# Four-layer transformer on one core: the fourth layer's after-attention work moved into its attention loop, and three projections restaged chunk by chunk

## The chip, the cores and the metric

The kernel runs on one core of one Trainium2 chip. The metric is the time of one execution in microseconds (us) of the device. Engines are named as the profile names them: PE is TensorE, DVE is VectorE, ACT is ScalarE, POOL is GpSimd and SP is SyncE, which here only issues DMAs.

## The reference

Four pre-norm layers over x of shape (4, 1024, 128): a batch of 4, 1024 tokens each, 128 features. Each layer is `x = x + attention(layernorm(x))` and then `x = x + ffn(layernorm(x))`. The fourth layer, which changes most, computes:

```python
q, k = (x @ Wq.T), (x @ Wk.T)            # 8 heads x 2 halves x 8 features
v = x @ Wv.T                             # 8 heads x 16 features
L1, L2 = l2norm(q1) @ l2norm(k1).T * cos_scale, l2norm(q2) @ l2norm(k2).T * cos_scale
G = tanh(delta_gain * (L1 - L2))
y = (softmax(L1 + G) - lambda_full * softmax(L2 - G)) @ v
y = y * rsqrt(mean(y * y over 16) + 1e-5) * subln_weight * 0.5
x = x + y @ Wo.T + bo
# ffn: top-1 of 8 experts, capacity S // E, first come first served
gates = softmax(layernorm(x) @ wg); expert = argmax(gates)
pos = cumsum(one_hot(expert)) - 1; keep = pos < C
out = (relu(xe @ w1 + b1) @ w2 + b2)[slot] * gate
```

The first layer has causal attention of 16 heads, the second an attention with a gain and biases before and in its projection, the third a causal attention of 8 heads and a top-1 mixture of experts like the fourth's.

## The kernel before, in words

x stays in SBUF as `x_sb`, 32 tiles of 128 tokens. Work runs in blocks (`nc.Block()`), each with one hand-written instruction list per engine; the order of every queue is the order in the code, and counting semaphores tie the lists together. A block ends when all its engines have ended. Stages around the change:

- `project` (L114), layers 1 and 2. A loop over four batches; each has two chunks of 512 tokens. DVE normalises the chunks (L107), PE turns them (four transposes), ACT copies them out, PE makes the q and the k product of a chunk (L213) and the v products. Each product is split into three bf16 parts: DVE copies it from PSUM with its bias to `val` (L283, L287), ACT makes the high part (L242), DVE the remainder `val - high` (L295), ACT the middle part (L245), POOL the low part (L259). SP stores parts (L184) and the padded values `vpad` (L187). DVE starts the norms of batch 0 after waiting for all weights and POOL's `vpad` presets.
- `project_cosine` (L1472), layer 4: the same with a third product and l2 norms. A batch's four q and k products are squared by ACT (L1578), summed by DVE (L1612), rooted by ACT (L1580), refined by DVE (L1624 to L1636), turned by PE (L1565), and only then the six splits of that batch run (`val` L1647 and L1649, L1585, L1655, L1588, L1600, stores L1522 and L1525). ACT alternates between Copy/Square (L1575, L1578) and Sqrt (L1580), one set of table loads each batch.
- `cosine_attention` (L1664), layer 4. 256 steps: 4 batches x 4 groups of heads x 2 halves of queries x 8 key blocks. A step s: PE makes the product of the difference (L1757 `a_diff_ps`), ACT takes tanh (L1805 `a_gate`), PE makes two logit products (`a_logit_ps`), DVE adds or subtracts the gate (L1852, two instructions), ACT takes exp of all four tiles a step later (L1811), PE multiplies with v two steps later (L1781). Every eighth step DVE copies the result out (L1847, a step with s % 8 = 2), PE turns it (L1791, s % 8 = 3) and DVE normalises it (L1832, L1834, L1840, s % 8 = 4) into `nat`. Batch 0 is unrolled, batches 1 to 3 are one `Fori(1, BATCH)` whose body is 64 steps.
- Behind it, each for all 32 tiles at once: `out_project` (L1281: square L1355, mean L1374, root, scale L1384, turn, product with Wo L1347, bias L1389, add to x L1395, statistics L42), `layer_stats` (L45), `route` (L1862: transposes L1889, router product L1900), `assign_slots` (L2279), `send_rows` (L2386: 32 indirect DMAs by POOL, L2409, and the load of the expert weights), then `switch_experts` (rows loaded at L2457).
- Layer 3's `row_attention` (L445) already does the same chain for a batch during the next batch's steps (product L608, choice L842 to L852, slots L858 to L880, scatters L643). Its steps are unrolled.

Of the kernel before, what the change touches and what calls it, by code (L numbers as in the profile page):

```python
# [8 lines left out]
U32 = mybir.dt.uint32  # L9
ALU = mybir.AluOpType  # L10
# [11 lines left out]
KB = T // P  # L22
GROUPS = 4
# [90 lines left out]
def project(nc, name, src, mv, rstd, wq, wk, wv, qs, ks, vs, ident, heads, v_width,  # L114
            gain=None, qk_bias=None, v_bias=None, pos=None):

    q_tiles = wq.shape[1] // P
    items = 2 * q_tiles
    vdim = wv.shape[1]
    hd = vdim // heads
    v_items = vdim // P
    with ExitStack() as ctx:
# [9 lines left out]
        w_qk = sb("w_qk", [P, items, P])  # L138
        w_v = sb("w_v", [P, vdim])
        xn = [sb(f"xn{i}", [P, CH]) for i in range(2)]  # L140
        xnT = sb("xnT", [P, 2, CH])
        NB = 4
        val = [sb(f"val{i}", [P, CH]) for i in range(NB)]
        rem = [sb(f"rem{i}", [P, CH]) for i in range(NB)]
        parts = [sb(f"parts{i}", [P, 3, CH], BF16) for i in range(NB)]
        vpad = [sb(f"vpad{i}", [P, CPT, heads, v_width]) for i in range(2)]
        gain_sb = sb("gain_sb", [P, 2])
        bias_sb = sb("bias_sb", [P, items])
        vb_sb = sb("vb_sb", [P, vdim])
        pos_sb = sb("pos_sb", [P, T])  # L150
# [3 lines left out]
        xn_done = sem("xn_done")  # L154
        loaded, xT_ready, xT_done = sem("loaded"), sem("xT_ready"), sem("xT_done")
        item_ready, val_done, hi_done = sem("item_ready"), sem("val_done"), sem("hi_done")
        rem_done, mid_done, lo_done = sem("rem_done"), sem("mid_done"), sem("lo_done")
        v_ready, v_done, v_preset = sem("v_ready"), sem("v_done"), sem("v_preset")
        stored = [sem(f"stored{i}") for i in range(NB)]
        v_stored = [sem(f"v_stored{i}") for i in range(2)]  # L160
        n_loads = 3 + sum(a is not None for a in (gain, qk_bias, v_bias, pos))
# [3 lines left out]
        def _(sp):  # L165
            sp.dma_start(w_qk[:, 0:q_tiles, :], wq.rearrange("c (n d) -> c n d", d=P)).then_inc(loaded, 16)
# [6 lines left out]
            if v_bias is not None:  # L173
                sp.dma_start(vb_sb[:], v_bias.to_broadcast([P, vdim])).then_inc(loaded, 16)
            if pos is not None:
                sp.dma_start(pos_sb[:], pos).then_inc(loaded, 16)
# [2584 lines left out]
```

## Time and profile before

| | |
|---|---|
| median of 3 runs | 3845.98 us (3845.41 to 3851.53) |
| profiled execution, its own time | 3840.85 us |
| span in the profile | 3839.1 us, mean granted clock of PE 0.89 |
| PE busy | 3039.5 us (79%) |
| DVE busy | 2681.6 us (70%) |
| ACT busy | 2180.8 us (57%) |
| POOL busy | 285.7 us (7%) |

Shares of the whole span say little here, since the stages have different limits; the stages the change touches lie in these stretches (us from the span's start):

| stretch | stage |
|---|---|
| 35.5 to 108.9 | `project` of layer 1 |
| 971.0 to 1044.2 | `project` of layer 2 |
| 2704.2 to 2829.3 | `project_cosine` |
| 2829.3 to 3603.8 | `cosine_attention` |
| 3603.8 to 3741.7 | its last turn, then `out_project` to `send_rows` |
| 3741.7 to 3839.1 | `switch_experts` of layer 4 |

A row of the timeline has start, duration, engine, line, operation, out<-in and count; a bracket at the end has the engine's idle time before it and what ended that. `PEld` is the loading of weights into PE, which overlaps its matmuls.

### The profile page before, as it was taken

Reading aid. Unit: us, or ns where it says so; the run is one execution under the profiler, and the core shown is the slowest. Engines: PE = TensorE matmul, PEld = TensorE weight load, DVE = VectorE, ACT = ScalarE, POOL = GpSimd, SP = SyncE. Lnnn points to the kernel's source line nnn. Section 1 sums busy time; section 2 is a strip of 40 time slices with the busy share of each in tenths; the row PEclk is TensorE's granted clock in tenths of the full one; section 3 lists DMA queues with packets and bytes.
Section 4 is the critical chain, followed back from the end, with each engine's and each line's share of the span. In section 5 each row is a group of like instructions: output and inputs, shape, how many; then the busy total and the mean of one; then the engine's idle time right before and its main releaser. Section 6 shows DMA issues by size and latency. Waiting matters only on the chain. (4 is left out here: it accounts for less than half of the span.)

```text
span 3839.1 us, 54232 instructions
## 1 busy us (share of the span) xinstructions
PE 3039.5 (79%) x18410; PEld 1243.4 (32%) x18410; DVE 2681.6 (70%) x5914; ACT 2180.8 (57%) x2753; POOL 285.7 (7%) x347
## 2 busy tenths in 40 slices
PE   3699996796499999996599999956339998989626
PEld 2233334342212222223355555544312222222224
DVE  5799983445599999993566666631658888888721
ACT  2266664222237777775255545522349999999602
POOL 2000000000200000000000000013120000000033
PEclk8699997898669999998699999978669999999858
DMA  6432210000422111200000000012253222220022
GB/s 228 100 54 47 47 26 2 21 0 0 164 49 36 35 29 32 40 1 5 28 1 1 1 6 3 5 52 66 74 110 53 31 31 31 31 31 1 2 72 86
DMA packets 159647, 156.48 MB, mean 41 GB/s; under 512 B 46424, under 2 KB 126056, under 8 KB 156848
## 3 DMA queue, kind: packets, MB, share of 16 engines
q1 hardware_dynamic: 155312, 145.57, 17.6%
q0 software_dynamic: 4096, 7.78, 0.6%
q8 instruction: 144, 2.36, 0.3%
q14 instruction: 95, 0.78, 0.1%
HBM read 91.17 MB, written 62.00 MB: 40 GB/s over the span
## 5 line engine op out<-in xcount | busy, mean ns | idle before, releaser
L1197 ACT ACTIVATE a_probs<-a_scores 128x1024 f32<-128x1024 f32 (+3 forms) x896 | 791.9, 933 | 397.4 <-PE a_scores L1094 247.6
L1220 DVE TENSOR_REDUCE a_part_max<-a_slot_ps 128x1 f32<-128x512 f32 x1280 | 798.6, 684 | 40.3 <-PE a_slot_ps L1072 38.8
L1852 DVE TENSOR_TENSOR a_probs<-a_logit_ps,a_gate 128x1024 f32<-128x1024 f32 x512 | 603.0, 1220 | 116.9 <-ACT a_gate L1805 116.9
L1072 PE MATMUL a_slot_ps<-a_k_op,a_q_op 48*128 48x512 bf16 (+3 forms) x1792 | 579.8, 380 | 113.5 <-DMA a_k_op<-scratch_k 51.6
L1811 ACT ACTIVATE a_probs<-a_probs 128x2048 f32<-128x2048 f32 x256 | 487.7, 1905 | 0.7 <-DVE a_probs L1852 0.7
L1094 PE MATMUL a_scores<-a_q_op,a_k_op 51*128 51x512 bf16 (+3 forms) x1792 | 453.2, 362 | 7.3 <-ACT a_probs L1197 6.1
L1114 PE MATMUL a_o_ps<-a_probs,a_v_op 128*32 128x512 f32 (+3 forms) x3584 | 438.0, 561 | 1.2 <-ACT a_o_sb L1184 0.6
L1072 PEld LDWEIGHTS a_slot_ps<-a_k_op,a_q_op 48*128 48x128 bf16 x1792 | 150.4, 94 | 715.5 <-DVE a_part_max L1220 468.9
L1757 PE MATMUL a_logit_ps<-a_q_op,a_k_op 96*128 96x512 bf16 x1024 | 303.5, 384 | 63.1 <-DVE a_probs L1852 51.3
L1805 ACT ACTIVATE a_gate<-a_diff_ps 128x1024 f32<-128x1024 f32 x256 | 261.2, 1020 | 60.4 <-PE a_diff_ps L1757 49.9
L1781 PE MATMUL a_o_ps<-a_probs,a_v_op 128*32 128x512 f32 x2048 | 274.5, 608 | 2.6 <-ACT a_probs L1811 2.0
L1216 DVE CUSTOM_DVE_ANT_0 a_slot_ps<-a_slot_ps,a_mask_wide 128x128 f32<-128x128 f32 (+3 forms) x512 | 237.0, 516 | 14.2 <-PE a_slot_ps L1072 13.2
L670 ACT ACTIVATE a_turned_sb<-a_turn_ps 128x512 f32<-128x512 f32 x192 | 93.6, 487 | 211.2 <-PE a_turn_ps L545 210.6
L660 ACT ACTIVATE space<-space,a_lows 128x128 f32<-128x128 f32 (+7 forms) x256 | 195.2, 768 | 4.0 <-DVE a_lows L754 4.0
L1757 PE MATMUL a_diff_ps<-a_qd_op,a_k_op 96*128 96x512 bf16 x512 | 156.2, 387 | 41.9 <-DMA a_v_op<-scratch_v 37.3
L545 PE MATMUL a_turn_ps<-ident_sb,space 128*128 128x128 f32 x1152 | 168.0, 278 | 21.6 <-DVE a_turned_sb L765 16.9
L765 DVE COPY a_turned_sb<-a_turn_ps 128x512 f32<-128x512 f32 x192 | 106.7, 556 | 94.7 <-PE a_turn_ps L545 94.2
L754 DVE CUSTOM_DVE_ANT_0 space<-a_score_ps,a_mask 128x512 f32<-128x512 f32 (+3 forms) x256 | 138.6, 587 | 37.7 <-PE a_score_ps L532 37.5
L1757 PEld LDWEIGHTS a_logit_ps<-a_q_op,a_k_op 96*128 96x128 bf16 x1024 | 78.7, 97 | 251.8 <-DVE a_probs L1852 206.4
L545 PEld LDWEIGHTS a_turn_ps<-ident_sb,space 128*128 128x128 f32 x1152 | 133.3, 142 | 69.3 <-issue 32.1
L532 PE MATMUL a_score_ps<-a_kT,a_qT 64*128 64x512 f32 (+3 forms) x768 | 153.2, 519 | 1.1 <-DVE a_lows L754 1.0
L559 PE MATMUL a_o_ps<-a_turned_sb,a_v 128*64 128x512 f32 (+3 forms) x768 | 149.6, 511 | 0.0
(398 smaller groups left out, 3782.5 us busy)
## 6 DMA issues: line engine op xcount, KB each, us to landing
a_q_op<-scratch_q SPq DMA_DIRECT2D x576, 32.0 KB
a_k_op<-scratch_k SPq DMA_DIRECT2D x576, 32.0 KB
scratch_v<-p_vpad SPq DMA_DIRECT2D x16, 1024.0 KB, 4.6
a_v_op<-scratch_v SPq DMA_DIRECT2D x32, 512.0 KB, 6.4
scratch_q<-p_parts SPq DMA_DIRECT2D x24, 384.0 KB, 2.6
scratch_k<-p_parts SPq DMA_DIRECT2D x24, 384.0 KB, 2.6
a_qd_op<-scratch_g SPq DMA_DIRECT2D x192, 32.0 KB
slots<-zero_slots SPq DMA_DIRECT2D x2, 2080.0 KB, 8.7
```

Source lines behind the costliest of these rows:

```text
L545: mm = nc.tensor.transpose(turn_ps[j][:, t * P:(t + 1) * P], rows_of(u, h, t)[0][:, j, kb * P:(kb + 1) * P], ident[:])
L1072: nc.tensor.matmul(out[:, 0:width], q_op[g][r0:r0 + MAX_ROW, e, qt * P:(qt + 1) * P], k_op[g][r0:r0 + MAX_ROW, e, kh * CH:kh * CH + width] ...
L1094: return nc.tensor.matmul(scores[e][:, jj, off:CH], k_op[g][r0:r1, e, kb * P:(kb + 1) * P], q_op[g][r0:r1, e, hq * CH + off:(hq + 1) * CH] ...
L1114: mm = nc.tensor.matmul(o_ps[32 * j:32 * (j + 1), off:CH], v_op[g][:, kb, 32 * j:32 * (j + 1)], probs[(u * S + n) % NB][:, j, off:CH], sta ...
L1197: nc.scalar.activation(probs[gs % NB][:, 2 * e:2 * e + 2, off:CH], scores[e][:, :, off:CH], ACT.Exp, scale=scale).then_inc(probs_done, 1)
L1216: nc.vector.tensor_tensor_reduce(out=slot[:, 0:w], in0=slot[:, 0:w], in1=mask_wide[:, CH - w:CH], scale=1.0, scalar=-3e38, op0=ALU.add, op ...
L1220: nc.vector.tensor_reduce(part_max[u % 2][:, kh, col:col + 1], slot[:, 0:w], axis=AX.X, op=ALU.max).then_inc(slot_done, 1)
L1757: mm = nc.tensor.matmul(out[:, j, :], ops[g][0][:, j, kb * P:(kb + 1) * P], q[:, j, hq * CH:(hq + 1) * CH], start=True, stop=True)
L1781: mm = nc.tensor.matmul(o_ps[c0:c0 + 32, :], v_op[g][:, kb, j * 32:(j + 1) * 32], probs[s2 % 4][:, m, j, :], start=kb == 0, stop=kb == KB - 1)
L1805: nc.scalar.activation(gate[s % 2][:], diff_ps[:], ACT.Tanh).then_inc(gate_done, 1)
L1811: nc.scalar.activation(tile[:], tile[:], ACT.Exp).then_inc(exp_done, 1)
L1852: nc.vector.tensor_tensor(probs[s % 4][:, m, :, :], logit_ps[m][:], gate[s % 2][:], op) \
```

## The change

1. `project`: no loops. The steps of chunk c and the transposes of chunk c + 2 are interleaved. The copy to `val` is gone: ACT makes the high part straight from PSUM (with the bias), DVE the remainder from PSUM. `parts` has 8 buffers for 4, `vpad` 4 for 2 (POOL presets four). DVE makes the norms of four chunks before it waits for the presets and the weights.
2. `project_cosine`: the same, with products, squares, roots and norms of chunk c + 1 made while chunk c is split. One Sqrt and its reciprocal and refinement for each chunk (128 elements) where there was one for each batch (256).
3. `cosine_attention`: the loop over batches is unrolled to 256 steps and 64 more behind them. At step r of the next batch, work of the finished batch runs: DVE means at r = 7, PE turns at 13 and 15 (ACT copies a step later), PE products with Wo at 17 and 20, DVE adds to x at 18 and 21, statistics at 19 and 22, moments at 23, PE turns at 30 and 32, router product at 34, DVE choice at 35, 37, 38, ACT exp at 36, PE counts at 39, DVE slots at 40 to 43. All PE tasks of this kind and the turns of L1791 share one PSUM bank, `spare_ps`. POOL adds the output bias to all of x at the start and, for each batch, squares, takes the inverse roots (17 small instructions each, twice), scales, makes the eight normalised row tiles and issues the eight scatters.
4. `out_project`, `layer_stats`, `route`, `assign_slots` and `send_rows` of layer 4 are gone. The expert weights load into the space of the attention's operands of groups 0 and 1 once the last batch has left them.

The core of the diff (of project: one product; of the attention: the new lists):

```diff
 def project(...):
-                for n in range(2 * items + 1):
-                        nc.scalar.activation(parts[n % NB][:, 0, :], val[n % NB][:], ACT.Copy).then_inc(hi_done, 1)
+            for c in range(CHUNKS):
+                high(2 * c)
+                if c > 0:
+                    middle(2 * c - 1)
+                high(2 * c + 1)
+                middle(2 * c)
+                if c + 2 < CHUNKS:
+                    take(c + 2)
+            for c in range(4):
+                norm(c)
+            dve.wait_ge(v_preset, 8)
             dve.wait_ge(loaded, 16 * n_loads)
+            for c in range(CHUNKS):
+                remainder(2 * c)
+                remainder(2 * c + 1)
+                values_out(c)
+                if c + 4 < CHUNKS:
+                    norm(c + 4)
 def project_cosine(...):   # DVE
+            for c in range(CHUNKS):
+                if c + 1 < CHUNKS:
+                    sums(c + 1)
+                remainder(ITEMS * c)
+                if c + 3 < CHUNKS:
+                    norm(c + 3)
+                remainder(ITEMS * c + 1)
+                if c + 1 < CHUNKS:
+                    units(c + 1)
+                remainder(ITEMS * c + 2)
+                if c + 1 < CHUNKS:
+                    values_out(c + 1)
 def cosine_attention(...):
-            steps(0, range(NS))
-            with te.Fori(1, BATCH) as b:
-                steps(b, range(NS))
+            for gs in range(shape.END):
...
+                for task in shape.tasks(gs):
+                    spare(task)
+        at = {13: ("t", 0), 15: ("t", 1), 17: ("y", 0), 20: ("y", 1), 30: ("x", 0), 32: ("x", 1), 34: ("l",), 39: ("n",)}
+            def inverse_root(v, y, y0, trial, factor):   # POOL
+                root(nc.gpsimd.tensor_scalar(first, bits, -0.5, float(0x5f3759df), ALU.mult, ALU.add))
+                for i in range(4):
+                    root(nc.gpsimd.tensor_tensor(trial, y0, y0, ALU.mult))
+                    root(nc.gpsimd.tensor_tensor(trial, trial, v, ALU.mult))
+                    root(nc.gpsimd.tensor_scalar(trial, trial, -0.5 * last, 1.5 * last, ALU.mult, ALU.add))
+                    root(nc.gpsimd.tensor_tensor(y if i == 3 else y0, y0, trial, ALU.mult))
+            for b in range(BATCH):   # POOL
+                pool.wait_ge(nat_done, 2 * GROUPS * (b + 1))
+                nc.gpsimd.tensor_tensor(square[:], rows, rows, ALU.mult).then_inc(squared, 1)
+                pool.wait_ge(mean_done, b + 1)
+                inverse_root(mean[:], inv[:], guess[:], trial[:], 0.5)
+                nc.gpsimd.tensor_tensor(groups, groups, inv[:].unsqueeze(2).to_broadcast([P, NG, RMS]), ALU.mult).then_inc(scaled, 1)
+                pool.wait_ge(moments, b + 1)
+                inverse_root(var[:], rstd[:], var_guess[:], var_trial[:], 1.0)
+                for t in range(KB):
+                    ins = nc.gpsimd.tensor_scalar(xr[:, t, 0:D], x[:, tile * D:(tile + 1) * D], mv[:, t, 0:1], rstd[:, t:t + 1], ...)
+                pool.wait_ge(slot_done, b + 1)
+                for t in range(KB):
+                    nc.gpsimd.indirect_dma_start(out=slots, ...).then_inc(sent[b], 16)
 def four_layers(...):
-                out_project(nc, "o3", nat, D, a["L3_Wo"], x, stats, consts, bias=a["L3_bo"], rms=(16, 1e-5, 0.5, a["L3_subln"]))
-                layer_stats(nc, "f3n", x, mv, rstd, dst=xn, stats=stats)
-                route(nc, "f3r", xn, a["L3_wg"], EXPERTS, logits, ident)
-                assign_slots(nc, "f3a", logits, descending[EXPERTS], a["before_me"], gate, slot_in)
-                send_rows(nc, "f3s", xn, slot_in, gate, a["token_ids"], slots[1], sent, weights.load)
```

## Rows read from the trace of the kernel before

**Rows 1.** Windows, one for each stage: busy us of each engine (x instructions).

```profile
core 0: us, PE busy (x) PEld busy (x) DVE busy (x) ACT busy (x) POOL busy (x), PEclk, DMA share, GB/s
35.50:108.90 73.40, 38.43 (x128) 23.21 (x128) 40.74 (x72) 23.90 (x41) 23.86 (x21) 0.78 0.60 225
971.00:1044.20 73.20, 38.76 (x128) 23.33 (x128) 41.63 (x72) 25.43 (x40) 24.08 (x20) 0.69 0.55 204
2704.20:2829.30 125.10, 51.59 (x288) 46.13 (x288) 91.44 (x144) 55.70 (x85) 35.48 (x29) 0.61 0.32 111
2829.30:3603.80 774.50, 679.75 (x3708) 163.15 (x3708) 649.07 (x638) 712.32 (x513) 10.50 (x6) 0.98 0.23 31
3603.80:3741.70 137.90, 34.45 (x198) 32.51 (x198) 52.50 (x159) 17.70 (x22) 30.98 (x32) 0.58 0.17 50
3741.70:3839.10 97.40, 65.56 (x352) 45.47 (x352) 17.34 (x28) 25.98 (x40) 31.09 (x32) 0.83 0.30 86
```

**Rows 2.** Timeline of the attention: tanh gates eight steps apart, and the turn.

```profile
3044.41 1.02 ACT L1805 ACTIVATE a_gate<-a_diff_ps 128x1024 f32<-128x1024 f32 x1 [0.20 <-PE a_diff_ps L1757]
...
3047.12 1.01 ACT L1805 ACTIVATE a_gate<-a_diff_ps 128x1024 f32<-128x1024 f32 x1
...
3049.41 0.66 PE L1791 MATMUL a_turn_ps<-ident_sb,a_o_sb 128*128 128x128 f32 x4
...
3050.53 1.02 ACT L1805 ACTIVATE a_gate<-a_diff_ps 128x1024 f32<-128x1024 f32 x1 [0.59 <-PE a_diff_ps L1757]
...
3067.47 1.02 ACT L1805 ACTIVATE a_gate<-a_diff_ps 128x1024 f32<-128x1024 f32 x1
```

**Rows 3.** The same view of the stores of the first projection.

```profile
50.00:106.00 56.00, 31.56 (x108) 19.06 (x106) 36.71 (x62) 21.56 (x37) 19.97 (x16) 0.73 0.67 252
```

**Rows 4.** Tiles of the projections: ns min/median/max, first and last start.

```profile
L295 DVE TENSOR_TENSOR p_rem<-p_val,p_parts x32: 675/681/1464, 49.4 to 1032.9; 128x512 f32<-128x512 f32 x32
L1655 DVE TENSOR_TENSOR p_rem<-p_val,p_parts x24: 674/834/1636, 2726.3 to 2820.2; 128x512 f32<-128x512 f32 x24
...
L312 DVE TENSOR_TENSOR p_vpad<-p_v_ps,p_vb_sb x8: 678/684/693, 984.8 to 1034.3; 128x512 f32<-128x512 f32 x8
...
L1575 ACT ACT_TABLE_LOAD  x4: 1283/1283/1283, 2704.8 to 2794.0; - x4
```

**Rows 5.** Groups of lines between the attention and the experts' first load.

```profile
L2409 POOL DMA_INDIRECT slots<-f_xn,f_slot_in x32 | 31.0, 968 | 866.0 <-DVEq L2388 856.5 <-issue 9.1 <-DMA slots<-f_xn,f_slot_in 0.3
...
L1347 PE MATMUL o_y_ps<-o_w,o_natT 128*128 128x128 f32 x64 | 9.4, 296 | 3.0 <-DVE x_sb L1395 3.0
```

**Rows 6.** Timeline of layer 3's attention: the same tasks done within its steps.

```profile
2506.85 0.87 DVE L42 BATCH_NORM_STATS2 stats<-x_sb 128x6 f32<-128x128 f32 x4
...
2529.00 1.95 PE L608 MATMUL a_spare_ps<-a_w_r,a_xrT 128*128 128x8 f32 x16
...
2530.99 0.23 DVE L842 COPY a_logits<-a_spare_ps 128x64 f32<-128x64 f32 x1 [2.98 <-PE a_spare_ps L608]
...
2533.61 0.20 DVE L852 RECIPROCAL a_gate<-a_best 128x8 f32<-128x8 f32 x1
...
2538.34 0.23 DVE L858 COPY a_count<-a_spare_ps 128x64 f32<-128x64 f32 x1 [3.21 <-PE a_spare_ps L613]
...
2543.11 0.17 DVE L880 CAST a_slot_in<-a_slot 128x8 uint32<-128x8 f32 x1
```

**Rows 7.** Timeline of the attention where the loop turns over.

```profile
3225.39 0.11 PEld L1757 LDWEIGHTS a_diff_ps<-a_qd_op,a_k_op 96*128 96x128 bf16 x2 [3.39 <-issue]
```

**Rows 8.** Groups of POOL's lines: busy us, mean ns | idle before.

```profile
L1173 POOL TENSOR_TENSOR a_neg_rem<-a_neg_max,a_max_parts 32x128 f32<-32x128 f32 x32 | 13.3, 417 | 2.5
L2238 POOL TENSOR_TENSOR f_kact<-f_relu 128x512 f32<-128x512 f32 x8 | 8.3, 1039 | 121.9 <-ACT f_relu L2229 121.9
```

**Rows 9.** Timeline at the end of the scatters.

```profile
3735.79 0.97 POOL L2409 DMA_INDIRECT slots<-f_xn,f_slot_in  x1 [0.30 <-issue]
```

**Rows 10.** Windows: a long stretch of layer 3's attention, whose steps are unrolled.

```profile
1906.00:2500.00 594.00, 563.47 (x3380) 328.36 (x3382) 389.21 (x1212) 331.42 (x793) 15.72 (x16) 0.98 0.01 3
```

More of the change, by code:

```diff
@@ L9 @@
 U32 = mybir.dt.uint32
+I32 = mybir.dt.int32
 ALU = mybir.AluOpType
@@ L22 @@
 KB = T // P
+EXPERTS = 8
+CAP = TOK // EXPERTS
+HID = 512
 GROUPS = 4
@@ new lines, in take @@
+            def take(c):
+                act.wait_ge(xT_ready, c + 1)
+                if c >= 4:
+                    act.wait_ge(v_ready, c - 3)
+                if gain is None:
+                    nc.scalar.activation(xnT[c % 4][:], t_ps[c % 2][:], ACT.Copy).then_inc(xT_done, 1)
+                else:
+                    nc.scalar.activation(xnT[c % 4][:], t_ps[c % 2][:], ACT.Identity, bias=gain_sb[:, 1:2],
+                                         scale=gain_sb[:, 0:1]).then_inc(xT_done, 1)
@@ L1497, in project_cosine @@
-        val = [sb(f"val{i}", [P, CH]) for i in range(NB)]
-        rem = [sb(f"rem{i}", [P, CH]) for i in range(NB)]
-        parts = [sb(f"parts{i}", [P, 3, CH], BF16) for i in range(NB)]
+        xn = [sb(f"xn{i}", [P, CH]) for i in range(3)]
+        xnT = [sb(f"xnT{i}", [P, CH]) for i in range(3)]
+        square = [sb(f"square{i}", [P, CH]) for i in range(2)]
+        ss, root, newton = (sb(n, [P, 2, groups]) for n in ("ss", "root", "newton"))
+        unit = [sb(f"unit{i}", [P, CH]) for i in range(2)]
@@ new lines, in middle @@
+            def middle(n):
+                act.wait_ge(rem_done, n + 1)
+                nc.scalar.activation(parts[n % RING][:, 1, :], rem[n % RING][:], ACT.Copy).then_inc(mid_done, 1)
+            take(0)
+            squares(0)
+            take(1)
+            roots(0)
+            for c in range(CHUNKS):
+                if c + 1 < CHUNKS:
+                    squares(c + 1)
+                high(ITEMS * c)
+                if c + 2 < CHUNKS:
+                    take(c + 2)
+                high(ITEMS * c + 1)
+                middle(ITEMS * c)
+                if c + 1 < CHUNKS:
+                    roots(c + 1)
+                high(ITEMS * c + 2)
+                middle(ITEMS * c + 1)
+                middle(ITEMS * c + 2)
@@ new lines, with __init__, where, after @@
+class CosineShape:
+    S = 2 * KB
+    NS = GROUPS * S
+    TOTAL = BATCH * NS
+    END = TOTAL + NS
+    def __init__(self):
+        self.place = {}
+        for gs in range(self.END):
+            for task in self.tasks(gs):
+                self.place[task] = len(self.place)
+    def where(self, gs):
+        b, s = divmod(gs, self.NS)
+        return b, s // self.S, s % self.S // KB, s % KB
+    def after(self, gs):
+        b, r = divmod(gs, self.NS)
+        return b - 1, r
+    def tasks(self, gs):
+        if gs % KB == 3 and KB <= gs < self.TOTAL + KB:
+            yield "o", gs // KB - 1
+        b, r = self.after(gs)
+        at = {13: ("t", 0), 15: ("t", 1), 17: ("y", 0), 20: ("y", 1), 30: ("x", 0), 32: ("x", 1), 34: ("l",), 39: ("n",)}
+        if b >= 0 and r in at:
+            yield (at[r][0], b, *at[r][1:])
```

1200 lines of the change are left out of this document (633 added, 567 removed).

## The prediction

> **What bounds the kernel now.** I cut the span into stages first [rows 1], since each has its own limit, then read in each which engine is never idle. The profiled run took 3840.85 us, 1.75 more than its span, and lies 5.1 below the median of 3845.98; the sum is made against the profiled run, and its result is taken as it stands. A difference below about 0.2% (8 us) can't be told from none.
>
> *Attention, 774.5 us* [rows 1]: PE is busy 679.75, ACT 712.32, DVE 649.07. The gates of eight steps, of which one has the turn, are 23.06 us apart, 2.88 a step [rows 2]. Two gates with ACT never idle between them are 2.71 apart, so ACT is the limit with PE close behind: where PE has the turn besides (0.66), ACT waits 0.59 for the next difference, and that step grows from 2.71 to 3.41 [rows 2]. DVE's 649.07 over 256 steps are 2.54, and about 2.38 without the work of every eighth step, so it has some 0.44 of slack against the 2.81 of an ordinary step ((23.06 - 3.41) / 7). 256 steps of 2.88 are 737; the other 37 are start, end and turns of the loop.
>
> *Projections, 73.4, 73.2 and 125.1 us* [rows 1]: nothing is full. The busiest engine is DVE, 40.74 of 73.4 and 91.44 of 125.1: these stages are a chain that passes from engine to engine. The DMA share in the stretch of stores is 0.67 of 56 us, that is 37.5 us of full share [rows 3].
>
> *After the attention, 137.9 us* [rows 1]: no engine is busy more than 52.5. It is a chain too, over all 32 tiles.
>
> **Part 1, projections of layers 1 and 2.** A batch loses four `val` copies of DVE, each as long as L295, 0.68 [rows 4], and the order in which the turn, products and splits of one batch follow each other. What is left for a chunk is: DVE two remainders, the values and four norms, 3 x 0.68 + about 1.5 (40.74 less 8 x 2 x 0.68 copies, over 8 chunks, is 3.7 [rows 1, 4]) = about 3.8; ACT 23.90 / 8 = 3.0; PE 38.43 / 8 = 4.8; DMA 37.5 / 8 = 4.7 [rows 1, 3]. The largest is 4.8; I take 5.2, since a full queue of stores never closes up wholly. Before, the chunks took about 7.0 (56 / 8 [rows 3]). That is 8 x 1.8 = 14.4 less. The norms of four chunks and two of PE's turns now stand before the wait for the weights, so the first store comes earlier, by 0 to 4.6; POOL's presets, four for two, are in its way, and I take 1. Each projection gains 15.5, the two 31. Ends: at a chunk of 5.5 and nothing at the start 12 each; at 4.8 and 2.4 at the start 20 each. Range -24 to -40 (rival B goes further).
>
> A rule of the Trainium skill bears on this ("SBUF — State Buffer", section "SBUF: two separate sides"): a DVE instruction with two SBUF inputs and a GpSimd instruction that reads SBUF shut each other out for their whole length. The trace agrees: L295 and L1655 (two SBUF inputs) go from 0.68 up to 1.46 and 1.64, while L312, with one input in PSUM, never leaves 0.68 to 0.69 [rows 4]. By this rule the new remainders, which read PSUM, never stretch, and the sum would get 24 x 0.16 = 4 us more in the third projection; my sum leaves that out.
>
> **Part 2, projection of layer 4.** The four table loads of 1.28 at L1575 [rows 4] become one pair each chunk instead of each batch, if the list alternates; at most 16 x 1.28 - 8 x 1.28 = 10 more on ACT and at least 0, and hidden as long as ACT has room: ACT's 55.7 over eight chunks is 7.0, with loads 8.3 to 9.6. DVE's 91.44 less 24 `val` copies of 0.70 is 74.6, or 9.3 a chunk [rows 1, 4]. The two pass work to each other, so I take 9.9 (before, the loads lie 89.2 us apart over three batches [rows 4], 14.9 a chunk). The stage is then 12 for the first norms, product, square, root and unit, 8 x 9.9 = 79 of chunks and 6 for the last parts and stores: 97 for 125.1, -28. Ends: at 11.5 a chunk -15; at 8.9, with no stretched remainder, -36.
>
> **Part 3, the attention.** Each of three batches adds to the 64 steps of the next:
> - PE: four turns of 0.66 [rows 2], two products with Wo of 1.17 (9.4 / 8 [rows 5]), the router's 1.95 [rows 6] and the counts, about 0.3: 7.2 us. A turn of 0.66 cost 0.59 of the step, 0.9 for each us: 6.4.
> - ACT: four copies of 0.6 (the size of 512 columns) and one exp of 0.26: 2.7. They fall one step behind the PE task, when ACT has some idle time from it: 1.5 counted.
> - DVE: means about 1.3, two adds of 0.68, eight statistics 1.74 and moments 0.9 [rows 6], choice 2.8 (2530.99 to 2533.81) and slots 4.9 (2538.34 to 2543.28) [rows 6]: 12.9. They lie in some 14 steps with 0.44 of slack each; over the slack are 7.4, half of which coincides with PE's and ACT's delays: 3.7.
> - POOL: nothing else waits for it there but step 13's turn (it has six steps, 17 us, for square, root and scale) and step 30's.
>
> Sum 11.6, for three batches +34.5. Ends: 0 (all falls into slack), and all three lists added without overlap, 16.5 x 3 = 49. The eight steps with DVE's slots (r = 40 to 43) are queued ahead of L1852, for which PE's next logits and ACT's exp wait. The loop went round twice, and at each PE stood for 3.39 us on nothing the trace shows [rows 7]: with the steps unrolled that goes, -7. Net +27.5, from -7 to +42.
>
> New waits elsewhere: SP loads the constants behind the first four groups' operands, hidden for 64 steps; the weights now load during the last batch (DMA share 0.23 [rows 1]), hidden. POOL's four bias adds are at the start of the attention, where it only had 10.5 us of work [rows 1]; if `biased` came late, step 18 would be late, some 180 us after.
>
> **Part 4, the end.** The 137.9 us from the last L1781 to the first load of expert rows [rows 1] become one batch's chain: last copy, turn and normalise 2.6; square of 1024 elements on POOL 2 x 1.04 = 2.1 [rows 8]; means 1.4; 17 steps of the root at 64 elements, each between L1173's 0.42 for 128 [rows 8] and nothing: I take 0.35, 6.0; scale 2.3; turns, ACT copies, products, adds, statistics, moments about 11 [rows 2, 5, 6]; root of 8 elements 17 x 0.23 = 3.9; eight row tiles 3; turns, router 7.2; choice, exp, counts and slots 2.8 + 4.9 + 0.3 [rows 6] = 7.9; eight scatters of 1.27 (0.968 and 9.1 / 32 idle [rows 5]) = 10.2; the end of the block 4.9 (from the end of the last scatter, 3736.8, to 3741.7 [rows 1, 9]). Sum 62.9, so -75. Ends: steps of the root at 0.6 and cold PE, -62; at 0.2, -85.
>
> A second rule speaks against the change. The Trainium skill ("GPSIMD Engine Reference", section "3. Performance versus the Vector engine") has GpSimd take about twice VectorE's time for the same elementwise work and advises leaving it there. The trace shows 1.04 for 512 elements on POOL [rows 8] beside 0.68 on DVE [rows 4]. By that rule the last chain would be about 5 us shorter with DVE doing POOL's part, but in each of three running batches DVE would get 12 us more.
>
> `switch_experts`, 97.4 us [rows 1], stays as it is.
>
> **The sum.** -31 - 28 + 27.5 - 75 = -106.5; 3840.85 - 106.5 = 3734.4. For what no row prices (starts of the projections, the end of the longer unrolled lists) I give 5 us back: 3739.
>
> **Rivals.**
> - B. *The projections stay bound by PE and the DMA queue.* The clock granted in these stages was 0.78, 0.69 and 0.61 [rows 1]; PE's 4.8 us a chunk were made at 0.78; all at the 1.2 GHz level they would be 4.8 x 0.78 / 0.5 = 7.5, as long as the chunk takes now, and half way the two stages and the third gain 28 for 59. Against: PE is less idle than before. Time 3739 + 31 = 3770.
> - C. *The attention hides all added steps.* For: DVE's and ACT's mean use is 84% and 92% [rows 1]. Against: the turn, 0.66 of PE, was not hidden [rows 2]. Time 3739 - 34 = 3705.
> - D. *POOL's small instructions take about 1 us each with their own waits.* 34 of them: the scale is late for step 13 and holds PE's list, whose turn is ahead of the next differences (+5 in each of 3 batches), and the end grows by 23. Against: L1173 ran at 0.42 with 2.5 us idle in 32 [rows 8]. Time 3739 + 38 = 3777.
> - E. *POOL's long instructions hold DVE's up in the attention.* 4 bias adds, 4 squares and scales and 32 row tiles are some 40 us; if they doubled each L1852 they meet, +50 to +80: 3790 to 3820. Against: L312 never stretched beside POOL, and L1852 has one input in PSUM like it [rows 4].
> - F, the other side. *The instructions of the unrolled steps can't be fetched fast enough.* The loop body of 64 steps becomes 256 of them; the price is a stall on PE or ACT in each step. It decides from 0.45 us a step (256 x 0.45 = 115, more than the 106.5 gained); at 0.5 the time is 3860. Against: layer 3's attention is unrolled, and PE was busy 563.47 of 594 us there [rows 10].
>
> **How the numbers follow.** Forecast 0.59, B 0.16, C 0.11, D 0.07, E 0.05, F 0.02. The predicted time is the forecast's, 3739. Its own bounds: the ends of the terms, added as independent (8, 11, 25 and 12 on average to a side, root of the squares 31), give 3708 to 3770. With B, C and most of D taken in the range is 3702 to 3778; E and F are left out. Faster by more than 0.2% are all cases but F and a remnant of E: 0.97; within 0.2%: 0.01; slower: 0.02.
>
> **What would show it.** In the trace after: projections of about 58, 58 and 97 us in the stage windows, no table loads by the batch but by the chunk, remainders at 0.68 to 0.75; steps of batches 1 to 3 at 2.88 except r = 13 to 23 and 30 to 44, whose gates are 0.4 to 1.3 us further apart; no stall of PE between batch 1 and 2; from the last L1781 to the first load of expert rows about 63 us. Wrong I would be by a projection with PE idle and the DMA share near 0.9 (B), POOL's steps near 1 us (D), L1852 above 1.3 us while POOL works (E), or "issue" idle on each step (F).

## The result, and the profile after

The changed kernel takes 3753.01 us (median of 4 runs, 3743.57 to 3754.39) against 3848.63 before: ratio 0.9747, 95% interval 0.9728 to 0.9765, 95.6 us less. The forecast was 3739. Its profiled execution took 3752.66, span 3750.9, mean granted clock 0.904.

The windows of the stages in the profile after; columns as in [rows 1], which they answer row by row (the last one begins with the last step's end; the experts are in the table alone):

```profile
core 0: us, PE busy (x) PEld busy (x) DVE busy (x) ACT busy (x) POOL busy (x), PEclk, DMA share, GB/s
35.50:93.00 57.50, 28.37 (x128) 18.79 (x128) 32.42 (x56) 21.53 (x40) 26.44 (x24) 0.83 0.77 287
954.50:1011.80 57.30, 27.08 (x128) 18.01 (x128) 32.17 (x58) 24.26 (x40) 26.53 (x24) 0.74 0.71 261
2680.60:2775.40 94.80, 47.50 (x288) 44.09 (x288) 74.89 (x144) 43.57 (x82) 30.49 (x29) 0.75 0.40 147
2775.40:3587.80 812.40, 700.97 (x3858) 179.04 (x3858) 681.51 (x808) 723.10 (x528) 99.08 (x166) 0.97 0.27 37
3587.80:3653.70 65.90, 13.49 (x54) 10.76 (x54) 13.37 (x60) 2.82 (x5) 26.25 (x52) 0.51 0.02 7
```

| stage | before | after | difference | forecast |
|---|---|---|---|---|
| projection, layer 1 | 73.4 | 57.5 | -15.9 | -15.5 |
| projection, layer 2 | 73.2 | 57.3 | -15.9 | -15.5 |
| projection, layer 4 | 125.1 | 94.8 | -30.3 | -28 |
| attention, layer 4 | 774.5 | 812.4 | +37.9 | +27.5 |
| end of attention to first expert rows | 137.9 | 65.9 | -72.0 | -75 |
| experts, layer 4 | 97.4 | 97.2 | -0.2 | 0 |
| layer 3's attention and send (same code) | 693.5 | 702.9 | +9.4 | 0 |

The rest is 1 us; the sum is the difference of the spans, 88.2. The last line is in neither the change nor the forecast; it covers the 7.4 us by which the spans differ less than the medians do. The experiments come back to it.

In the attention, the three places where most is lost in a batch are steps 35, 36 and 46, about 1.5 us each (timeline after, in the third batch's steps, with the second batch's tasks). The first two:

```profile
3293.20 1.95 PE L2030 MATMUL a_spare_ps<-a_w_r,a_xrT 128*128 128x8 f32 x16
...
3295.64 1.02 ACT L2078 ACTIVATE a_gate<-a_diff_ps 128x1024 f32<-128x1024 f32 x1 [1.56 <-PE a_diff_ps L1984]
...
3299.24 0.66 PE L2010 MATMUL a_spare_ps<-ident_sb,a_o_sb 128*128 128x128 f32 x4 [1.78 <-DVE a_logits L1804]
...
3300.37 1.02 ACT L2078 ACTIVATE a_gate<-a_diff_ps 128x1024 f32<-128x1024 f32 x1 [1.91 <-PE a_diff_ps L1984]
```

The router's 16 products stand in PE's list ahead of the next difference, so tanh waits 1.56 us for it. A step later PE wants to turn the attention's own result (L2010) and finds the shared bank still holding the logits, which DVE copies (L1804) only behind its two L2222: PE stands 1.78 us, and with it the next difference. That is a new wait. It stands in the view of waits too, three times, once a batch. The line shown behind it also comes once a batch, at step 43: PE's product with v waits for DVE's copy of the result (L2215), which stands behind the slots' work.

```profile
PE a_spare_ps L2010 <- DVE a_logits L1804: 5.3, 3, 1.8
PE a_o_ps L1997 <- DVE a_o_sb L2215: 3.1, 3, 1.0
```

At step 46 it is DVE again: ACT's exp waits 1.35 us for the additions of the gate (L2222), which stand behind the last slots. At step 48 tanh begins 1.17 us late, though its product had ended at 3338.8 (PE's timeline) and ACT's exp at 3338.7: a stop with no wait of the kernel behind it.

```profile
3331.04 1.91 ACT L2083 ACTIVATE a_probs<-a_probs 128x2048 f32<-128x2048 f32 x1 [1.35 <-DVE a_probs L2222]
...
3339.89 1.02 ACT L2078 ACTIVATE a_gate<-a_diff_ps 128x1024 f32<-128x1024 f32 x1 [1.17 <-PE a_diff_ps L1984]
```

### The profile page after: what moved, and what is told of

It reads as the page before. It is cut to its first block and busy times, and to the rows that moved or that the text cites. A ratio compares the mean times of both kernels' runs of the same rounds, so it can differ in the third digit from the quotient of the medians.

```text
span 3750.9 us, 52502 instructions
## 1 busy us (share of the span) xinstructions
PE 3018.3 (80%) x18416; PEld 1226.5 (33%) x18416; DVE 2639.2 (70%) x5952; ACT 2160.9 (58%) x2748; POOL 369.7 (10%) x535
## 5 line engine op out<-in xcount | busy, mean ns | idle before, releaser
L2222 DVE TENSOR_TENSOR a_probs<-a_logit_ps,a_gate 128x1024 f32<-128x1024 f32 x512 | 602.0, 1218 | 121.7 <-ACT a_gate L2078 118.2
L1048 PEld LDWEIGHTS a_slot_ps<-a_k_op,a_q_op 48*128 48x128 bf16 x1792 | 150.3, 94 | 735.0 <-DVE a_part_max L1196 468.8
L1984 PE MATMUL a_logit_ps<-space 96*128 96x512 bf16 x1024 | 303.0, 386 | 74.5 <-DVE a_probs L2222 63.5
L1984 PE MATMUL a_diff_ps<-space 96*128 96x512 bf16 x512 | 156.9, 388 | 34.2 <-DMA a_v_op<-scratch_v 34.1
L730 DVE CUSTOM_DVE_ANT_0 space<-a_score_ps,a_mask 128x512 f32<-128x512 f32 (+3 forms) x256 | 138.5, 587 | 38.7 <-PE a_score_ps L508 38.4
L1984 PEld LDWEIGHTS a_logit_ps<-space 96*128 96x128 bf16 x1024 | 76.7, 98 | 267.9 <-DVE a_probs L2222 216.1
```

The source lines that it names most:

```text
L1048: nc.tensor.matmul(out[:, 0:width], q_op[g][r0:r0 + MAX_ROW, e, qt * P:(qt + 1) * P], k_op[g][r0:r0 + MAX_ROW, e, kh * CH:kh * CH + width] ...
L1984: mm = nc.tensor.matmul(out[:, j, :], ops[g][0][:, j, kb * P:(kb + 1) * P], q[:, j, hq * CH:(hq + 1) * CH], start=True, stop=True)
L2222: nc.vector.tensor_tensor(probs[gs % 4][:, m, :, :], logit_ps[m][:], gate[gs % 2][:], op) \
```

## The experiments

All are compared with the kernel before on the same chip, where its median was 3848.07 for the first four, 3836.97 for the next four, 3849.68 for the following three and 3850.32 for the last. "Extra per batch" is taken from the starts of the 256 tanh gates: the time from the gate before, less that between the same two positions of eight in a stretch without tasks (together 23.07 us for eight steps in every kernel here), summed over a batch's 64 steps.

**Each part alone.** The kernel before, with one function of the change put in.

```diff
-def project(...):          # before
+def project(...):          # changed, nothing else
```

> The kernel before with the changed project of layers 1 and 2 and nothing else. Theory: each of the two stages takes what it takes in the changed kernel, about 57.3 us for 73.3, because the stores' queue is then the limit; nothing else moves: 32 us less, near 3814. A second question: layer 3's attention, whose code is the same in both kernels, took 9.3 us longer in the changed kernel, with PE at its lower clock level in stretches where it had the higher one before. If that is tied to the shift in time that the first two projections make, it shows here too and the gain is only 23 us; if it is tied to the fourth layer's part, it is absent here.

Measured: 3814.11 (3813.53 to 3814.93), ratio 0.9912 (0.9896 to 0.9929), 34.0 less.

```diff
-def project_cosine(...):   # before
+def project_cosine(...):   # changed, nothing else
```

> The kernel before with the changed project_cosine alone. Theory: 94.8 us for 125.1 in that stage, with one Sqrt table load in place of eight loads: 30 us less, near 3816. Rival: part of that gain came from the stages in front being shorter (a shifted clock): then less than 25 us.

Measured: 3817.80 (3815.92 to 3821.28), ratio 0.9923 (0.9906 to 0.9939), 30.3 less.

```diff
-cosine_attention, out_project, layer_stats, route, assign_slots, send_rows of layer 4   # before
+cosine_attention of the change, both projections left as before
```

> The kernel before with the changed attention of the fourth layer and all that follows it, but both old projections. Theory: from the attention's start to the first load of expert rows 878 us for 912, so 34 us less, near 3812; the three single parts then add up to the whole change (32 + 30 + 34 = 96) but for layer 3's 9 us. Rival: the parts overlap, and the sum of the three is more than 5 us away from that.

Measured: 3812.26 (3810.33 to 3813.32), ratio 0.9906 (0.9890 to 0.9923), 35.8 less. The three gains are 34.0 + 30.3 + 35.8 = 100.1, the whole change brings 95.6: the parts add up within the 5 us set as the bound, and the intervals (about 6 us each) are wide enough for all of that difference.

The second question of the first run has the answer that neither theory had: layer 3's attention with its scatters (from its first product to the first load of rows) took 703.9 us in the run with the projections, 703.8 in each of the next two, which hardly shift it in time, and 700.9 in the one with the loop unrolled. It was 693.5 in the profile of before and 702.9 after. So it isn't the change; the profiled execution of before was a quick one.

**The loop of the attention unrolled, nothing else.**

```diff
-            with te.Fori(1, BATCH) as b:      # PE; ACT's, DVE's and the loads' loop the same way
+            for b in range(1, BATCH):
                 steps(b, range(NS))
```

> The kernel before with the three lists of the attention loop (PE, ACT, DVE) and the loads' loop unrolled, every instruction the same. Theory: the two turns of the loop cost 3.5 to 4 us each, so 7 to 8 us less in the gates from first to last (742.5 before, 735 here); the 44 us more that the changed kernel's gates show against that are the after-attention tasks and batch 0. Rival F of the prediction: code of 256 unrolled steps can't be fetched fast enough, then the gates take longer than before.

Measured: 3839.56 (3836.12 to 3841.99), ratio 0.9979 (0.9970 to 0.9989). First to last gate: 735.0 us for 742.5, 7.5 less, where the forecast had 7. Rival F is out: an unrolled list isn't slower by the step. In PE's waits over the gates the two waits for issue of together 4.6 us (2.5 at the turn of [rows 7]; its 3.39 is the idle time of PE's weight loads, not of its products) are absent; the first line of what is left:

```profile
PE a_logit_ps L1757 <- DVE a_probs L1852: 48.4, 133, 0.5
```

The trace of before says more of the turn. From 3219 to 3226 us the view of DMAs has nothing but two packets of the kind "instruction", 16 KB each, at 3222.5 and 3225.9; PE stands from 3222.9 to 3225.4. In all six turns of the three traces that have the loop there is such a pair, 3.1 to 3.4 us apart, and in the unrolled one there is none. That agrees with code being brought in where the loop turns; it doesn't prove that PE waits for it.

**PE's tasks behind the next difference.**

```diff
                     product(diff_ps, ops[g][1], gs).then_inc(diff_ready, 1)
+                for task in shape.tasks(gs - 1):
+                    spare(task)
                     for m in range(2):
                         product(logit_ps[m], ...)
                 values(gs - 2)
-                for task in shape.tasks(gs):
-                    spare(task)
```

DVE's normalise goes behind its L1852 of the same step.

> The changed kernel with PE's after-attention tasks and turns put behind the next step's difference instead of ahead of it, and DVE's normalise behind its L1852. Theory: 13.4 us more a batch are mostly PE tasks that hold the next difference, and so the next tanh (the 1.5 us at step 35 is the router's 1.95), and one hold-up by the shared bank at step 36. Behind the difference they run while ACT works: about 6 of the 13.4 us a batch go and part of the 0.34 a turn over an ordinary step, 20 to 28 us in all, near 3728. Rival: DVE's additions are the price; then the tasks only move the wait from ACT's tanh to DVE's L1852 and less than 8 us go.

Measured: 3727.25 (3726.18 to 3732.64), ratio 0.9714 (0.9698 to 0.9730). On this chip that is 12.6 us less than the changed kernel's ratio gives (0.9747 x 3836.97 = 3739.9); from the first gate to the last it takes 765.5 us where the two runs of this chip with the old order take 776.3 and 776.7. Extra per batch: 10.0 us for 13.4 to 13.7 in those two (13.4 to 14.6 in the first profile after, up to 16.2 when the changed kernel was run again). So the direction is right and the size half: 3.5 us a batch went, not 6, and the turns didn't get cheaper at all (23.07 us for eight steps before and behind). What is left shows both causes; the table has the extra of the steps in one batch (the second with tasks), summed over those that differ by more than 0.15 us either way:

| steps | changed | other order | spread |
|---|---|---|---|
| 10 (means) | 0.7 | 0.9 | 0.4 |
| 14 to 22 (turns, Wo, adds, statistics) | 2.9 | 3.1 | 2.7 |
| of these, 22 | 0.2 | 2.5 | 2.1 |
| 31 to 37 (turns, router, choice) | 4.2 | 2.5 | 2.5 |
| 40 to 48 (slots) | 5.1 | 3.5 | 1.1 |
| of these, 48 (the stop) | 1.1 | 0 | 0 |

Step 22 is new: the second product with Wo now meets a bank that DVE frees only with the later normalise. The shared bank gives one such collision in either order. The stop of 1.1 us at step 48 is gone, and nothing in the order explains it: in the two old-order runs of this chip it lies at step 37 or 46 instead, once a batch. Of the 3.5 us saved, 1.1 are this stop.

**DVE's pieces spread.**

```diff
-                if r == 37: chooser.mark(...)       # 6 instructions
-                if r in (40, 41, 42, 43): chooser.assign(...)
+            CHORES = (6, 7, 18, 19, 20, 21, 22, 23, 25, 35, 37, 38, 39, 40, 41, 43, 45, 46, 47, 49)
+                if r in CHORES: next(chores)        # 20 pieces, at most 4 instructions each
```

> As the run with the other order, and DVE's after-attention work cut into 20 pieces on 20 steps, where it lay on 13 (slots: 8 pieces from step 40 to 49, not 4 to 43). Theory: what then is left of the 13.4 us a batch is DVE work above its slack of about 0.3 us a step; pieces half as long lose less of it: 2 to 4 us a batch less than the run with the order alone, 6 to 12 us. Rival: DVE's slack is gone once PE's tasks are hidden; then spreading changes less than 3 us.

Measured: 3720.31 (3716.90 to 3721.03), ratio 0.9694 (0.9678 to 0.9710), 6.9 less than the other order alone. Extra per batch 7.8 for 10.0. The slots, 5.1 us in the changed kernel with the stop and 3.5 in the other order, are down to 1.1: DVE has some slack at each step, and a piece that is longer than it costs the rest.

**The last batch's row work on DVE.**

```diff
-                ins = nc.gpsimd.tensor_scalar(xr[:, t, 0:D], ...)      # POOL, all batches
+                if b == BATCH - 1:                                      # DVE
+                    ins = nc.vector.tensor_scalar(xr[:, t, 0:D], ...)
```

The square and the scale of that batch go the same way.

> The changed kernel with the last batch's square, scale and eight row tiles on DVE, which is idle by then, and not on POOL. Theory, from rows of both: row tiles 6.2 us on POOL against 2.1 on DVE, scale 1.9 against 1.2, square 1.9 against 1.2: 5.5 us less between the attention's end and the first load of expert rows, near 3748. Rival: handing over between POOL and DVE costs as much as is gained; then no difference.

Measured: 3732.04 (3729.55 to 3739.62), ratio 0.9730 (0.9714 to 0.9746), which overlaps the changed kernel's. The stretch shows it without that spread: from the last gate to the first load of expert rows 66.7 us for 72.5, 5.8 less (72.1 in two other runs of this chip). POOL's row tiles in the changed kernel, then DVE's here (timelines):

```profile
3619.07 6.22 POOL L2136 TENSOR_SCALAR a_xr<-x_sb,a_mv,a_rstd 128x128 f32<-128x128 f32 x8
```

```profile
3600.99 2.14 DVE L2188 TENSOR_SCALAR a_xr<-x_sb,a_mv,a_rstd 128x128 f32<-128x128 f32 x8 [4.92 <-POOL a_rstd L2111]
```

**Is the store queue the limit of the projections?** One more store of the q parts.

```diff
                     sp.dma_start((qs, ks)[i][b, ...], parts[n % (2 * NB)][:])
+                    if i == 0:
+                        sp.dma_start(extra[b, ...], parts[n % (2 * NB)][:])
```

> The changed kernel with each q tile of the projections of layers 1 and 2 stored a second time, to a tensor that isn't used there: 384 KB more on the 1792 KB of a chunk, 21%. Theory: these stages are now as long as their stores take; each grows by 21% of some 40 us, 8 us, 16 us in all. Rival: the chain from engine to engine is still the limit and the queue has room: less than 3 us each.

Measured: 3757.18 (3753.65 to 3760.72), ratio 0.9789 (0.9770 to 0.9809). From its first norm to the next block's start the first projection takes 64.6 us where the other kernels of that chip took 56.3 to 57.2, the second 64.8 for 56.5 to 56.6; together that is 15.7 to 16.5 more, the forecast 16. The DMA share says the same, the changed kernel first, then with the extra store (windows of the stores, as [rows 3]):

```profile
50.00:92.00 42.00, 20.41 (x104) 13.52 (x102) 20.60 (x37) 18.35 (x35) 17.32 (x16) 0.77 0.94 350
```

```profile
50.00:99.00 49.00, 19.27 (x101) 12.99 (x99) 20.29 (x35) 17.56 (x34) 17.28 (x15) 0.74 1.00 364
```

Before, it was 0.67 over 56 us. The engines end their part some 18 us ahead of the stage (the last v copy ends at 74.5 us, the next block starts at 93.0).

**The changed kernel again, with two others.**

> The changed kernel again, on the same chip as the next two. Question: layer 3's attention took 693.6 us in the profile of before, 702.9 in that of the change, 704, 704, 704 and 701 in the four single parts, and 693 to 694 in four later variants of the change. If the chip or the execution decides this and not the kernel, all three runs of this call agree within 1 us, whatever the value. Against before on the same chip: 0.9747 as measured, between 0.973 and 0.977.

Measured: 3752.23 (3749.57 to 3755.05), ratio 0.9745 (0.9732 to 0.9758). Layer 3's attention: 705.3, 704.8 and 703.9 us in the three kernels of this chip, 702.8 in the one of the last chip, 700.9 to 703.9 in the first four, and 693.1 to 694.1 in all four of the chip of the other-order run. It goes with the chip (or the time of measuring; each was used once) and not with the kernel, and the medians of the kernel before go the same way: 11 to 13 us less on that chip.

The traces say where the time goes, if not why. Instruction by instruction on DVE, the nine slower traces keep pace with the five quick ones but for a few places, and three of these are in all nine: 336 to 341, 498 to 505 and 659 us from the first product, together 6.3 to 9.2 of the 7.8 to 12.2 us. Each is at or just behind the eight scatters of a batch. At the first, DVE stands 4.47 us where it stood 1.07 before, and the transfer named as its releaser, a store of a projection, had landed long ago. At the last, the 32 products with Wo take 5.95 us, most of it at PE's lower clock level, where they took 3.84 at the higher one before.

```profile
2208.68 0.69 DVE L741 COPY a_turned_sb<-a_turn_ps 128x512 f32<-128x512 f32 x1 [4.47 <-DMA scratch_q<-p_parts]
```

**The presets apart from the norms.**

```diff
+            pool.wait_ge(xn_done, 4)
             for vp in vpad:
                 nc.gpsimd.memset(vp[:], 0.0).then_inc(v_preset, 1)
```

> The changed kernel with POOL's presets in the projections of layers 1 and 2 started only when the four chunks' norms are done. In the changed kernel 16 norms beside the presets took 9.73 us, and the presets 1.94 each where they had taken 1.80. Theory: the two hold each other up; apart, 16 norms take 5.5 us or less and the presets 1.80, and the stage stays as long as it was (within 1 us), since its start waits for the weights and its length is that of the stores. Rival: the norms are slow for another reason and stay near 9.7.

The timeline of the changed kernel (its repeated run), then of this one:

```profile
35.73 7.47 POOL L251 MEMSET p_vpad<- 128x2048 f32 x4 [16.57 <-POOLq L53]
35.78 9.73 DVE L268 TENSOR_SCALAR p_xn<-x_sb,mv,rstd 128x128 f32<-128x128 f32 x16 [0.53 <-PEq L53]
```

```profile
35.64 4.19 DVE L269 TENSOR_SCALAR p_xn<-x_sb,mv,rstd 128x128 f32<-128x128 f32 x16 [0.53 <-PEq L53]
39.88 7.04 POOL L252 MEMSET p_vpad<- 128x2048 f32 x4 [20.87 <-DVE p_xn L269]
```

Side by side the 16 norms took 9.73 us, by themselves 4.19, and the presets 7.47 against 7.04. The stage ends at 91.7 us for 92.7: a microsecond, since its start waits for the weights. The single time, 3746.83 us, does not measure so little. The Trainium skill ("SBUF — State Buffer", section "SBUF: two separate sides") has a DVE instruction in a two-port mode and any GpSimd instruction shut each other out; norms that more than double beside presets agree with it, though no trace tells whether these norms run in that mode.

**All of it, with two re-timings.** The second product with Wo a step later, the router's products in two halves, the last batch's row work on DVE.

```diff
-        at = {..., 20: ("y", 1), ...}
+        at = {..., 21: ("y", 1), ...}
+                    if before >= 0 and step == 33:
+                        router(before, 0)          # tiles 0 to 3; 4 to 7 with the task at 34
```

> The run with the spread pieces, plus the last batch's square, scale and rows on DVE, plus two re-timings: the second product with Wo a step later (so that PE doesn't wait for the normalise that frees the shared bank: 2.1 us at step 22), and the router's 16 products in two halves on two steps (2.1 us at steps 36 and 37). Theory: 2 to 3 us a batch for the re-timings, 5.7 for the last batch: 12 to 15 us less than the spread run, 33 to 36 less than the changed kernel, a ratio to before near 0.966. Rival: the router's halves only divide the same delay; then 2 us a batch less of the gain.

Measured: 3740.62 (3736.32 to 3748.46), ratio 0.9714 (0.9701 to 0.9727). A miss: 0.966 was expected, and by ratio it is no faster than the spread run (0.9694, intervals overlap), though step 22's 2.1 us are gone and steps 36 and 37 lose 1.3 for 2.1. Extra per batch is 15.7, 12.6 and 12.0, of which 8.2, 5.4 and 4.9 lie in steps 53 to 55. Without those the three are 7.5, 7.2 and 7.1 for the spread run's 7.8: the re-timings brought 0.3 to 0.7 us a batch, not 2 to 3, since step 32 now loses 1.3 for 0.5 and step 35 another 0.6, as the rival had it. In steps 53 to 55 everything stands (the second of the three batches):

```profile
3348.96 1.02 ACT L2099 ACTIVATE a_gate<-a_diff_ps 128x1024 f32<-128x1024 f32 x1
...
3349.88 1.90 ACT L2104 ACTIVATE a_probs<-a_probs 128x2048 f32<-128x2048 f32 x1
...
3352.75 1.23 DVE L2300 TENSOR_TENSOR a_probs<-a_logit_ps,a_gate 128x1024 f32<-128x1024 f32 x1 [3.24 <-DMA f2e_back<-results]
3353.59 0.97 POOL L2166 DMA_INDIRECT slots<-a_xr,a_slot_in  x1 [0.30 <-issue]
3356.34 1.02 ACT L2099 ACTIVATE a_gate<-a_diff_ps 128x1024 f32<-128x1024 f32 x1 [4.55 <-DMA results<-f2e_res,f2e_dest]
```

The product of the difference began at 3351.1 (PE's timeline) and the gate starts 4.6 us after ACT's exp has ended. The releasers named are transfers of layer 3 that had landed long before, so the profile has no wait in this kernel to put it down to. At that time POOL's eight scatters, which spreading had moved to steps 50 to 52, ran together with the loads of the next batch; the DMA share from 3349 to 3357 is 0.68. It is the picture of layer 3's stops, and it comes on a chip where layer 3 has them too.

**The scatters earlier.**

```diff
-            CHORES = (..., 26, 35, 37, 38, 39, 40, 41, 43, 45, 46, 47, 49)
+            CHORES = (..., 25, 35, 36, 37, 38, 39, 40, 41, 42, 43, 45, 46)
-        at = {..., 39: ("n",)}
+        at = {..., 38: ("n",)}
```

> The re-timed kernel once more. In its trace all of PE, ACT and DVE stood still for 3 to 5 us at step 53 of each batch (ACT 4.55, DVE 3.24, with nothing waited for in the kernel), while POOL's eight scatters, started at step 49, and the loads of the next batch's third group ran. Here the slots are ready at step 46, not 49 (choice at 35 to 38, slots at 39 to 46), the moments are a step earlier, the rest is the same. Theory: the code of the unrolled lists is fetched through the same DMA engines and comes late where scatters and loads meet; with the scatters out of the loads' way the stop goes, 16 to 20 us of the run before, ratio to before near 0.966. Rival: the stop comes from where the code lies; then it stays at 3 to 5 us a batch at some step, wherever the scatters are, ratio 0.970 to 0.972.

Measured: 3732.74 (3728.81 to 3738.77), ratio 0.9694 (0.9681 to 0.9707): the best by ratio together with the spread run, 0.5% below the changed kernel's 0.9745 and clear of its interval. Between theory and rival: 0.2 points better than the run before, where the theory had 0.5, and the two intervals overlap a little. The stop is at most 2.3 us in a step now (steps 50 to 53, together 5.1, 5.6 and 2.1 us in the three batches) for 4.6 (8.2, 5.4 and 4.9 together). The stop moved with the scatters, which now start at step 47, and shrank; that the place of the scatters decides its size is likely, not shown, as the chip changed too. On the chip of the spread run the scatters lay at steps 50 to 53 without a stop above 0.6 us, and there layer 3 had no stops either.

That code is fetched late was only argued, and what the trace of the run before shows is against the simple form of it. Packets of the kind "instruction" are in the view of DMAs: one, of 1.2 us, ends as the second batch's stop begins (3350.6 to 3351.8), but there is none from 3147 to 3157 us and none from 3545 to 3553, around the first and the third batch's stops at step 53. How long such a packet waited before it started isn't recorded. The cause stays open.

## Why the prediction was right, and where it was off

**Baseline.** The sum was made against a profiled execution of 3840.85, 5 to 8 us below the medians of before; that was said, and "its result is taken as it stands". The runs show layer 3's attention at 701 to 705 us on most chips, where that execution had 693.5. Had the sum started from the median, the forecast would be 5 to 8 us higher, 3744 to 3747.

**The sum.** Measured 3753.0 for 3739, 14 more. Stage by stage, in the profiled executions: the attention 10.4 more than forecast and the end 3.0, the projections 3.1 less; layer 3's level 9.4, which no term had; and the 5 us given back "for what no row prices" hid 5 of it. No run shows anything at the starts of the projections or the end of the lists that those 5 would pay for; that they met part of the attention's miss is luck. Two sums in the text are off by a little: the end adds up to 62.5 and not 62.9, and 12.9 us of DVE less 14 times 0.44 are 6.7 over the slack and not 7.4.

**Part 1, projections of layers 1 and 2: right, by the named limit.** -15.9 each for -15.5. The period of a chunk was put at 5.2 with the DMA's 4.7 as the floor next to PE's 4.8; the stores took 42 us for eight, 5.25. PE fell off as a limit: 28.4 us busy for 38.4, or 3.5 a chunk, with 108 of its 128 matmuls begun at the higher clock level where it had been 66. The DMA share rose to 0.94, and the extra store, which lengthens the stages by its share of the bytes, shows that the stores set the length. The text took PE's 4.8 as the larger of the two; that the stores' floor was as high is why the number held, and that is partly luck. Rival B, PE at its lower clock level, is out for these stages. In the third the granted clock rose from 0.61 to 0.75, and PE is busy 47.5 of 94.8 us: it isn't the limit there either.

**Part 2, projection of layer 4: right in size, wrong in one step.** -30.3 for -28. The table loads were expected once a chunk; there is one in the whole stage, where before there were eight (four at L1575 and four at L1580):

```profile
L1577 ACT ACT_TABLE_LOAD  x1: 1283/1283/1283, 2690.0 to 2690.0; - x1
```

So Copy, Square and Sqrt can follow each other with one load here. The loads before went with the loop's body rather than with the change from one function to another; that is inferred, since no run unrolls that loop and nothing else. The remainders didn't stretch: 676 to 690 ns and 739 to 751 ns against 674 to 1636 before [rows 4]; a chunk took 9.6 us (from the first to the last Sqrt, 67.1 us over seven) for 9.9, which is the 2.3 us more.

**Part 3, attention: too small, and the terms wrong one by one.** +37.9 for +27.5. The turns of the loop brought 7.5 for 7. The tasks cost 14.6, 13.4 and 13.5 us in the three batches for 11.5, and 3.9 us more are in the unrolled first batch (187.8 us from its first gate to the next batch's for 183.9 before, 184.5 to 185.0 in six of the later runs), 2.2 of them in one step with PE at its lower clock. Going by what ACT waits for in each step, a batch of 13.4 divides like this (timeline after, the second batch with tasks; step 40 has a little of both PE and DVE). It is an attribution; the experiments bear on its PE and DVE parts:

| term | forecast | measured |
|---|---|---|
| PE's tasks ahead of the next difference (steps 14, 18, 21, 31, 33, 35) | 6.4 | 3.7 |
| ACT's copies and exp (15, 17, 32, 34, 37) | 1.5 | 1.8 |
| DVE's work (10, 22, 25, 40, 43, 45, 46) | 3.7 | 5.4 |
| the shared bank at step 36 | none | 1.5 |
| the stop at step 48 | none | 1.1 |

So the step that failed isn't PE's: a turn of 0.66 cost 0.2 to 0.5 and the router's 1.95 cost 1.5, less than the 0.9 of each microsecond that was counted. Mis-sized was DVE's term, since its work doesn't spread evenly over the slack of its steps (spreading it gave 2.2 us back); and the bank, which the text named nowhere as a wait, was left out. It asked what stands behind a waiting instruction on DVE, and not on PE. The stop could not have been read from the rows. "0.4 to 1.3 us further apart" held for eight of the named steps; 35 and 36 had 1.5, the others up to 0.3 or nothing, and 10, 25, 45, 46 and 48, which were not named, had 0.4 to 1.6. Rival C, all hidden, is out; rival E too: L2222 takes 1218 ns on the mean beside POOL's 99 us of work, as it took 1220 (L1852) beside 10.5 [rows 1], and no single one more than 1226.

**Part 4, the end: right.** 65.9 for 62.9. The root took 6.3 for 6.0, the second one 4.7 for 3.9. The mis-sized term is the eight row tiles, 6.2 for 3: 0.78 each, a form that [rows 8] don't have. Rival D is out: POOL's small steps are 0.25 to 0.32 us, with 0.08 between.

**The rule against the change** (the Trainium skill, "GPSIMD Engine Reference", section "3. Performance versus the Vector engine": GpSimd about twice as slow) holds for the last batch: three pieces moved to DVE saved 5.8 us, where the prediction put the whole at 5. The factor was 2.9 for the row tiles and 1.5 for the square. In the running batches POOL's share showed no cost of its own; that it would cost 12 us a batch on DVE wasn't tried.

## What to carry over

When work is put into the gaps of a running pipeline, place it in each list behind what the bound engine waits for next, cut it to the slack of one step, and look at each shared buffer for who frees it and how late. When a stage is a chain, ask what is the next limit before sizing the gain: here it was the stores. Divide a miss by what each engine waited for before naming the term that failed: the total hides terms that are off in both directions. And take the level of "before" from several executions: a single profiled one was 9 us quick in a stage that nobody touched.

## What the runs showed of the hardware

- A GpSimd preset and DVE norms from SBUF to SBUF hold each other up: 16 norms 9.73 us together, 4.19 apart; the four presets 7.47 and 7.04.
- POOL against DVE depends on the instruction: eight row tiles of 128 columns 6.22 against 2.14 us (2.9 times), a square of 1024 columns 1.89 against 1.22 (1.5 times).
- Two turns of a loop with 64 steps cost 7.5 us; in each of six turns in three traces two 16 KB packets of the kind "instruction" lie 3.1 to 3.4 us apart around it, and none such in the unrolled list.
- The same instructions of layer 3 took 693 to 694 us in four runs on one chip and in the profile of before, and 701 to 705 in the nine others; three of the places where the nine fall behind are in all of them, at or just behind eight scatters.
- All engines can stop for 1 to 5 us in an unrolled list with no wait of the kernel behind it. The long ones lie at scatters, and moved when the scatters did; on one chip they were absent. The cause is open.
